# First-unit queries and keys written on chip, a Newton inverse root on VectorE, and low parts of the second layer's up weights on GpSimd

## The chip, the cores and the metric

The kernel runs on one core of one Trainium2 chip. The metric is device time in microseconds (us). A core has five engines that run their own instruction streams in program order and meet only at semaphores: TensorE (PE, with weight loads shown as PEld), VectorE (DVE), ScalarE (ACT), GpSimd (POOL) and SyncE (SP, which here only issues DMAs).

## What is computed

Two transformer-like layers on x of shape 4 x 256 x 512, all in float32. Each layer normalises x, and adds to it an attention (32 query heads, 8 key heads, head size 16) and a feed-forward of the normalised x. Layer 0 has full attention and a GELU network of width 2048; layer 1 has causal attention with rotary embedding and a gated SiLU network of width 512.

```python
x = L0_attn_x
xn = _layernorm(x, axis=-1)
x = x + _L0_attn_ref(xn, L0_attn_Wq, L0_attn_Wk, L0_attn_Wv, L0_attn_Wo) + _L0_ffn_ref(xn, L0_ffn_W1, L0_ffn_fc1_bias, L0_ffn_W2, L0_ffn_fc2_bias)
xn = _layernorm(x, axis=-1)
x = x + _L1_attn_ref(xn, L1_attn_w_qkv, L1_attn_b_qkv, L1_attn_w_dense, L1_attn_b_dense) + _L1_ffn_ref(xn, L1_ffn_w12, L1_ffn_b12, L1_ffn_w3, L1_ffn_b3)

def _layernorm(x, axis=-1, eps=1e-05):
    m = jnp.mean(x, axis=axis, keepdims=True)
    v = jnp.var(x, axis=axis, keepdims=True)
    return (x - m) / jnp.sqrt(v + eps)
```

## The kernel before

**Precision by parts.** Each matmul operand of a projection or a feed-forward is kept as a rounded high part and a low part (the exact value minus the rounded one). `three` (L712) makes a product out of three matmuls. Weights arrive in pieces of 128x512: POOL issues the DMA into one of four `raw` buffers (L605), ACT casts it to the high part (L866, step "split"), and a subtraction makes the low part (step "low"). In layer 0 the subtraction for the pieces 0 to 23 of the up weights (`w_up`) is made by POOL (L644). All other low parts are made by DVE (L987). `low_on_dve` decides which engine it is. `w_up` has two slots, so an up piece is split shortly before TensorE needs it.

**Order.** `program_order` writes one list of steps; every engine walks through the list and carries out its own part of each step, in order. The work is cut into 32 units of 8 slots (`unit_slots`). A unit is a batch row n and one of four groups of 8 query heads; units 0 to 15 are layer 0, 16 to 31 layer 1. In a slot stand one step "st" (scores transposed, PE L792 or L795; exponential by ACT L931 into `probs`; in layer 1 a causal mask on `probs` by POOL, L654) and one step "m" for a later unit (scores, PE L766; their row maximum by DVE, L1086 or L1081). Around them the function `spread` deals out the projections, up, down and out matmuls (L712). "pv" (L814) multiplies probs by the values; it needs the masks of four slots. `followers` puts the "low" step one slot after its "split": for layer 1's up pieces, the split stands in slot 5 and the low in slot 6. "plus" (POOL L669) adds a bias into `x_res`, in units whose group is 3.

**Start.** ACT zeroes part of `q_sb` for the units 0 and 1 ("fill", L869, two casts of 32x2048), then takes the root of the variance. The layer norm is: "stats" on DVE (L997 to L1002), "root" on ACT (L876, Sqrt), "rstd" on DVE (L1008 to L1012, a reciprocal and one Newton step), "ln" on DVE (L1019). TensorE then transposes xn (L732). Keys and queries of batch row 0 go from the projection's bank to `stage`, by DMA to HBM ("store", L556 and L560), and by DMA into `q_sb` and `k_sb` ("load_q" L569, "load_k" L578); the scores of unit 0 wait for both.

**PSUM.** Five banks (`WORK_BANKS`) are handed round among m, qkv, up, down, wo and transposes. A bank comes free only when its reader (mostly DVE) is done.

## Time and profile before

| | |
|---|---|
| device time, median of 3 runs | 614.59 us (612.11 to 616.9) |
| time of the profiled execution | 612.6 us |
| span from its first to its last instruction | 610.8 us |
| PE busy | 568.8 us (93%) |
| PEld busy | 437.6 us (72%) |
| DVE busy | 452.1 us (74%) |
| ACT busy | 363.0 us (59%) |
| POOL busy | 232.5 us (38%) |
| mean granted TensorE clock | 0.989 |

PE is the engine with the least idle time, so what counts is what makes PE wait, and where its clock is granted at less than full. In the views below, a row of a timeline has the start, the duration, the engine, the line, the operation, the output <- the inputs, the shapes and the count; in square brackets stands how long the engine sat idle before it, and what ended that. Rows of the same operation that follow each other without a gap are merged. SPq and POOLq rows are DMA issues.

### The profile page before, as it was taken

The page shows a single profiled execution, that of the slowest core. Times are in us where ns is not written, and L with a number is a line of the kernel's source. Part 1 is how long each engine was busy: PE and PEld are TensorE (multiplying, and loading weights), DVE is VectorE, ACT ScalarE, POOL GpSimd, SP SyncE. Part 2 cuts the span into 40 slices and gives each one's busy share as a digit, 9 for nine tenths or more (in the row PEclk, how much of TensorE's full clock was granted, in tenths as well). Part 3 has the DMA queues.
Part 4 walks back from the last instruction along what each step waited for, and adds up shares of the span by engine and source line. Part 5 has one row for each costly group of instructions (what it writes and reads, how often), then busy time and mean ns, then how long its engine had stood idle before and what let it go on. Part 6 is the DMA issues. An engine that isn't in the chain of part 4 may idle for free.

```text
span 610.8 us, 10473 instructions
## 1 busy us (share of the span) xinstructions
PE 568.8 (93%) x3216; PEld 437.6 (72%) x3216; DVE 452.1 (74%) x1196; ACT 363.0 (59%) x615; POOL 232.5 (38%) x345
## 2 busy tenths in 40 slices
PE   2889899999999999999999998989889999999997
PEld 2786677787777878767777676857667777776764
DVE  5469867756565776476898677888988889798673
ACT  6448756754555674675684665447755664556461
POOL 6303334532303522213223114335755386455242
PEclk9989999999999999999999999979999999998999
DMA  5784632353223244316434324324543355444101
GB/s 190 224 252 129 172 90 68 105 156 105 69 87 105 71 120 140 87 35 173 122 122 121 87 57 118 88 76 120 151 107 88 81 160 143 104 123 105 35 2 69
DMA packets 30247, 68.07 MB, mean 111 GB/s; under 512 B 4848, under 2 KB 17648, under 8 KB 28144
## 3 DMA queue, kind: packets, MB, share of 16 engines
q1 hardware_dynamic: 21552, 39.09, 23.0%
q0 software_dynamic: 8640, 28.32, 15.8%
q8 instruction: 26, 0.43, 0.3%
q14 instruction: 29, 0.24, 0.1%
HBM read 52.44 MB, written 14.68 MB: 110 GB/s over the span
## 4 chain that ended last, share of the span: by engine, by line
PE 73%; ACT 7%; DVE 6%; issue 6%; POOL 5%; DMA 4%; ACTq 0%; SPq 0%; DVEq 0%; POOLq 0%
PE banks L712 50%; PE banks L766 7%; PE banks L792 7%; PE banks L814 6%; DMA q_sb<-max_t 1%; ACT L931 1%; POOL probs L654 1%; DVE banks L1081 1%; PE banks L795 1%; PE banks L732 1%; POOL raw L605 1%; ACT hid_f L951 1%; ACT L950 1%; DMA raw<-in_attn 1%; DMA q_sb<-q_parts 1%
## 5 line engine op out<-in xcount | busy, mean ns | idle before, releaser
L931 ACT ACTIVATE probs<-banks 128x512 f32<-128x512 f32 (+1 forms) x256 | 137.7, 546 | 175.7 <-PE banks L792 141.6
L712 PE MATMUL banks<-xnT,w_up 128*128 128x512 f32 x576 | 152.0, 397 | 1.6 <-issue 1.6
L1086 DVE TENSOR_REDUCE neg_max<-banks 128x2 f32<-128x512 f32 x128 | 87.4, 687 | 87.1 <-PE banks L766 86.7
L712 PE MATMUL banks<-w_down,hid 128*128 128x512 f32 x480 | 128.4, 401 | 4.5 <-ACT hid_f L951 2.0
L712 PEld LDWEIGHTS banks<-xnT,w_up 128*128 128x128 f32 x576 | 101.6, 189 | 29.2 <-issue 12.8
L766 PEld LDWEIGHTS banks<-k_sb,q_sb 96*128 96x128 f32 x512 | 94.3, 195 | 22.5 <-issue 4.1
L1081 DVE CUSTOM_DVE_ANT_0 banks<-banks,mask_qk 128x128 f32<-128x128 f32 (+1 forms) x256 | 86.3, 375 | 32.0 <-PE banks L766 31.9
L712 PEld LDWEIGHTS banks<-w_down,hid 128*128 128x128 f32 x480 | 85.5, 189 | 32.2 <-DVE neg_max L1086 7.5
L766 PE MATMUL banks<-k_sb,q_sb 96*128 96x256 f32 (+1 forms) x512 | 101.0, 279 | 4.7 <-DMA q_sb<-q_parts 3.0
L654 POOL TENSOR_SCALAR_AFFINE_SELECT probs<-probs 128x256 f32<-128x256 f32 x128 | 59.9, 468 | 89.2 <-ACT probs L931 83.1
L792 PE MATMUL banks<-q_sb,k_sb 97*128 97x512 f32 x192 | 80.0, 416 | 11.2 <-ACT probs L931 8.7
L712 PE MATMUL banks<-xnT,w_qkv 128*128 128x256 f32 x576 | 82.4, 291 | 1.6 <-DVE xnT L1025 1.4
L712 PEld LDWEIGHTS banks<-xnT,w_qkv 128*128 128x128 f32 x576 | 75.9, 196 | 4.4 <-DVE xnT L1025 1.8
L1125 DVE TENSOR_TENSOR x_res<-x_res,banks 128x512 f32<-128x512 f32 x96 | 63.7, 676 | 9.5 <-PE banks L712 9.5
L814 PE MATMUL banks<-probs,v_sb 128*32 128x512 f32 (+1 forms) x512 | 61.8, 555 | 1.2 <-POOL probs L654 1.2
L605 POOL DMA_DIRECT2D raw<-in_down x40 | 22.4, 561 | 100.8 <-DVE w_down L987 73.4
L644 POOL TENSOR_TENSOR w_up<-raw,w_up 128x512 fp32r<-128x512 f32 x24 | 32.4, 1350 | 73.3 <-ACT w_up L866 73.1
L792 PEld LDWEIGHTS banks<-q_sb,k_sb 97*128 97x128 f32 x192 | 36.5, 190 | 29.0 <-ACT probs L931 18.6
L712 PE MATMUL banks<-w_out,ctxT 128*128 128x512 f32 x192 | 50.8, 406 | 0.0
L605 POOL DMA_DIRECT2D raw<-in_up x48 | 27.1, 564 | 50.9 <-DVE w_qkv L987 21.6
L712 PEld LDWEIGHTS banks<-w_out,ctxT 128*128 128x128 f32 x192 | 35.1, 193 | 9.4 <-issue 2.9
L931 ACT ACT_TABLE_LOAD x29 | 37.2, 1283 | 0.5
(75 smaller groups left out, 663.1 us busy)
## 6 DMA issues: line engine op xcount, KB each, us to landing
q_sb<-q_parts SPq DMA_DIRECT2D x64, 256.0 KB, 4.5
raw<-in_up POOLq DMA_DIRECT2D x48, 256.0 KB, 3.2
raw<-in_down POOLq DMA_DIRECT2D x40, 256.0 KB, 3.0
q_parts<-stage SPq DMA_DIRECT2D x32, 256.0 KB, 2.5
raw<-in_attn POOLq DMA_DIRECT2D x20, 256.0 KB, 3.2
k_parts<-stage SPq DMA_DIRECT2D x16, 256.0 KB, 2.6
k_sb<-k_parts SPq DMA_DIRECT2D x16, 256.0 KB, 4.4
out<-x_res SPq DMA_DIRECT2D x8, 256.0 KB, 2.1
```

What stands on the lines that cost most here:

```text
L605: pool.dma_start(raw[:, k % RAW, :], src).then_inc(raw_loaded[k % RAW], 16)
L644: nc.gpsimd.tensor_tensor(to[1], raw[:, k % RAW, :], to[0].bitcast(F32), ALU.subtract).then_inc(lo_split_pool, 1)
L654: nc.gpsimd.affine_select(out=tri, in_=tri, compare_op=ALU.is_ge, fill=0.0, base=0, pattern=[[0, 2], [1, P]], channel_multiplier=-1).then_ ...
L712: mm = nc.tensor.matmul(out_ap, lhs(a), rhs(b_), start=first and j == 0, stop=stop and j == 2, **kw)
L732: mm = nc.tensor.transpose(banks[:, k, c * P:c * P + P], xn[:, t, c * P:c * P + P], ident[:, :])
L766: mm = nc.tensor.matmul(banks[:, k, r * T:r * T + w], q_sb[0:ROWS, u % RING, 2 * g + r, t * P:t * P + P], k_sb[0:ROWS, 4 * f + g, 0:w], st ...
L792: mm = nc.tensor.matmul(bank, keys, q_sb[0:MROW + 1, u % RING, 2 * g:2 * g + 2, :], start=True, stop=True)
L814: mm = nc.tensor.matmul(o, v_sb[:, t, 4 * f + g, :], p_, start=t == 0, stop=t == 1, skip_group_check=True)
L931: nc.scalar.activation(probs[:, i, 0:w], banks[:, ST_BANKS[k % 2], 0:w], ACT.Exp, scale=SCALES[n // B]).then_inc(exp_done, 1)
L1081: ins = nc.vector.tensor_tensor_reduce(out=scores, in0=scores, in1=mask_qk[:, T - w:], scale=1.0, scalar=3.0 * MASKED, op0=ALU.add, op1=AL ...
L1086: nc.vector.tensor_reduce(neg_max[:, s, 2 * g:2 * g + 2, t], banks[:, bank_of[x], :].rearrange("p (r t) -> p r t", r=2)[:, :, 0:w], AX.X, ...
L1125: nc.vector.tensor_tensor(x_res[:, tile, :], x_res[:, tile, :], banks[:, bank_of[y], :], ALU.add).then_inc(wk_emptied, 1)
```

## The change

- The first DMAs of keys and queries (stores of batch row 0, pair 2 and pair 0) go from `stage` straight into `k_sb` and `q_sb` (4 and 8 DMAs of 16 partitions x 8 x 256), instead of to HBM and back. "load_k" of row 0 and "load_q" of the units 0 and 1 are gone. Whoever used the HBM copies now waits for `first_k` and `first_q`.
- The fills of units 0 and 1 stand after the splits of the second pair of weight pieces, behind the first root.
- The root on ACT stays only for the first two layer norms. For the other six, DVE makes the inverse root alone: two integer instructions for a first guess and three Newton steps of three instructions.
- The low parts of all 16 up pieces of layer 1, and nothing else, move from DVE to POOL.
- POOL issues the weight loads 4 and 5 before its last three start-up instructions instead of after them.

```diff
 def start_slots():
-    o = [[("fill", 0), ("fill", 1), ("stats", 0, 0), ("root", 0, 0), ("rstd", 0, 0), ("ln", 0)] + split(0, "attn", 4, 5)]
-    o += [[("xn", 0, 0), ("xn", 0, 1)] + split(0, "attn", 0, 1)]
+    o = [[("stats", 0, 0), ("root", 0, 0), ("rstd", 0, 0), ("ln", 0)] + split(0, "attn", 4, 5)]
+    o += [[("xn", 0, 0), ("xn", 0, 1)] + split(0, "attn", 0, 1) + [("fill", 0), ("fill", 1)]]
...
-    o += [[("xn", 1, 0), ("xn", 1, 1), ("fill", 2), ("load_k", 0, 0), ("load_k", 0, 1), ("load_q", 0), ("load_q", 1)] + split(0, "up", 0, 1)]
+    o += [[("xn", 1, 0), ("xn", 1, 1), ("fill", 2)] + split(0, "up", 0, 1)]
...
-        slots[4] += [("root", 0, 2), ("root", 0, 3)]
...
-        slots[5].append(("root", 1, c))
...
-    return x[1] == 1 or x[2] != "up" or x[3] >= 24
+    return x[2] != "up" or x[1] == 0 and x[3] >= 24
...
+                    if x == ("store", 0, 2):
+                        for h in range(2):
+                            for e in range(2):
+                                at = 32 * h + 16 * e
+                                sp_.dma_start(k_sb[at:at + HD, :, :].bitcast(F32),
+                                              stage[:, k % 2, h, 0, :].bitcast(F32)).then_inc(first_k, 16)
+                    elif x == ("store", 0, 0):
+                        for j in range(2):
+                            for e in range(2):
+                                for h in range(2):
+                                    at = 32 * e + 16 * h
+                                    sp_.dma_start(q_sb[at:at + HD, j, :, :].bitcast(F32),
+                                                  stage[:, k % 2, h, j, :].bitcast(F32)).then_inc(first_q[j], 16)
...
             nc.gpsimd.memset(v_sb[:, :, :, :], 1.0).then_inc(made, 1)
             pool.wait_ge(made, ONES_V)
+            load(4)
+            load(5)
             nc.gpsimd.memset(k_sb[MROW:MROW + 1, :, :].bitcast(F32), 1.0).then_inc(made, 1)
...
-                        pe.wait_ge(q_loaded[u % RING], 32 * (u // RING + 1))
-                        pe.wait_ge(k_loaded[f], 16 * (n + 1))
+                        if u < 2:
+                            pe.wait_ge(first_q[u], 64)
+                        else:
+                            pe.wait_ge(q_loaded[u % RING], 32 * (u // RING + u % RING // 2))
...
+                if x[0] == "rstd" and ("stats",) + x[1:] not in stt:
+                    tiles = stat_tiles(x)
+                    t = slice(tiles[0], tiles[-1] + 1)
+
+                    link(nc.vector.tensor_scalar(dev[:, t].bitcast(I32), var_e[:, t].bitcast(I32), 1, None, ALU.arith_shift_right))
+                    link(nc.vector.tensor_scalar(rstd[:, t].bitcast(I32), dev[:, t].bitcast(I32), -1, GUESS, ALU.mult, ALU.add))
+                    for _ in range(3):
+                        link(nc.vector.tensor_tensor(rs0[:, t], rstd[:, t], rstd[:, t], ALU.mult))
+                        link(nc.vector.scalar_tensor_tensor(out=rs1[:, t], in0=rs0[:, t], scalar=-0.5, in1=var_e[:, t],
+                                                            op0=ALU.mult, op1=ALU.mult))
+                        link(nc.vector.scalar_tensor_tensor(out=rstd[:, t], in0=rs1[:, t], scalar=1.5, in1=rstd[:, t],
+                                                            op0=ALU.add, op1=ALU.mult))
```

The order of TensorE's instructions is the same before and after. Three places of the other engines follow.

ACT at the start of the program, before (`dev` is the root of the variance, `q_sb<-zero` are the fills):

```order
L869 ACT_TABLE_LOAD
L869 CAST q_sb<-zero 32x2048 x2
L876 ACT_TABLE_LOAD
L876 ACTIVATE dev<-var_e 128x2
L866 CAST w_qkv<-raw 128x512 x2
L884 CAST xnT<-banks 128x4x128 x2
```

and of the change:

```order
L913 ACT_TABLE_LOAD
L913 ACTIVATE dev<-var_e 128x2
L903 CAST w_qkv<-raw 128x512 x2
L921 CAST xnT<-banks 128x4x128 x2
L903 CAST w_qkv<-raw 128x512 x2
L906 CAST q_sb<-zero 32x2048 x2
L913 ACTIVATE dev<-var_e 128x2
```

The two fills and one table load have gone from ahead of the first root; the fills now stand ahead of the second one.

ACT in unit 16, the first of layer 1, before (L931 is the exponential of the scores):

```order
L969 CAST hid<-hid_f 128x512
L939 CAST ctxT<-o_t 128x256
L876 ACT_TABLE_LOAD
L876 ACTIVATE dev<-var_e 128x2
L866 CAST w_up<-raw 128x512
L931 ACT_TABLE_LOAD
L931 ACTIVATE probs<-banks 128x256 x2
```

and of the change:

```order
L1005 CAST hid<-hid_f 128x512
L975 CAST ctxT<-o_t 128x256
L903 CAST w_up<-raw 128x512
L967 ACTIVATE probs<-banks 128x256 x2
```

The root and both table loads around it are gone; the same happens in the units 0, 8, 12 and 20.

POOL at the end of unit 19, before (L654 is the mask, L676 the low part of the attention's output, L698 that of a key or query):

```order
L669 TENSOR_TENSOR x_res<-x_res,bias_out 128x512
L654 AFFINE_SELECT probs<-probs 128x256
L676 TENSOR_TENSOR ctxT<-o_t,ctxT 128x256
L654 AFFINE_SELECT probs<-probs 128x256
L605 DMA raw<-in_down 128x512
L654 AFFINE_SELECT probs<-probs 128x256
```

and of the change:

```order
L700 TENSOR_TENSOR x_res<-x_res,bias_out 128x512
L685 AFFINE_SELECT probs<-probs 128x256
L707 TENSOR_TENSOR ctxT<-o_t,ctxT 128x256
L685 AFFINE_SELECT probs<-probs 128x256
L675 TENSOR_TENSOR w_up<-raw,w_up 128x512
L634 DMA raw<-in_down 128x512
L685 AFFINE_SELECT probs<-probs 128x256
```

The low part of the next up piece stands in POOL's queue behind the mask of slot 6 and ahead of the mask of slot 7; before, DVE made it.

## Rows read from the trace of the kernel before

**Rows 1.** Waits of PE: who waited for whom, us in total, times, longest.
```profile
PE banks L792 <- ACT probs L931: 8.7, 6, 2.7
```

**Rows 2.** Timeline of the start: start us, us, engine, line, what.
```profile
2.10 3.69 ACT L869 CAST q_sb<-zero 32x2048 fp32r<-32x2048 f32 x2
...
5.30 0.17 DVE L1002 TENSOR_SCALAR var_e<-mv 128x2 f32<-128x2 f32 x1
...
5.81 1.28 ACT L876 ACT_TABLE_LOAD   x1
...
7.21 1.80 POOL L623 MEMSET k_sb<- 1x2048 f32 x1
...
7.93 1.11 DVE L1011 TENSOR_SCALAR rs<-rs 128x2 f32<-128x2 f32 x1
...
9.93 1.57 PEld L732 LDWEIGHTS banks<-ident,xn 128*128 128x128 f32 x8 [9.93 <-POOL mask_qk L625]
...
13.30 7.41 PE L712 MATMUL banks<-xnT,w_qkv 128*128 128x256 f32 x48 [1.40 <-DVE xnT L1025]
```

**Rows 3.** Timeline of the first scores (unit 0).
```profile
26.72 1.75 SPq L569 DMA_DIRECT2D q_sb<-q_parts  x4
...
32.34 0.47 PE L766 MATMUL banks<-k_sb,q_sb 96*128 96x256 f32 x2 [3.04 <-DMA q_sb<-q_parts]
...
38.34 0.52 PE L712 MATMUL banks<-xnT,w_qkv 128*128 128x256 f32 x3
...
38.94 1.56 PE L712 MATMUL banks<-xnT,w_up 128*128 128x512 f32 x6
```

**Rows 4.** Timeline of unit 0, slots 6 and 7.
```profile
57.72 1.28 ACT L876 ACT_TABLE_LOAD   x1
...
62.30 0.50 PE L792 MATMUL banks<-q_sb,k_sb 97*128 97x512 f32 x1 [2.40 <-ACT probs L931]
...
68.67 0.62 ACT L866 CAST w_out<-raw 128x512 fp32r<-128x512 f32 x1 [3.61 <-DMA raw<-in_attn]
```

**Rows 5.** Timeline of unit 16's end and unit 17's start.
```profile
395.81 1.28 ACT L876 ACT_TABLE_LOAD   x1
...
399.57 0.79 PE L792 MATMUL banks<-q_sb,k_sb 97*128 97x512 f32 x1 [2.69 <-ACT probs L931]
...
405.92 1.57 PE L712 MATMUL banks<-w_out,ctxT 128*128 128x512 f32 x6
```

**Rows 6.** Timeline of the same steps at unit 20's end, PE.
```profile
459.54 0.50 PE L792 MATMUL banks<-q_sb,k_sb 97*128 97x512 f32 x1 [0.67 <-ACT probs L931]
...
463.23 1.09 PE L712 MATMUL banks<-w_out,ctxT 128*128 128x512 f32 x4
```

**Rows 7.** Windows: us, busy (x) of PE, PEld, DVE, ACT, POOL, PEclk, DMA, GB/s.
```profile
34.00:36.00 2.00, 2.00 (x11) 2.00 (x10) 1.45 (x3) 0.00 (x0) 0.00 (x0) 0.50 0.82 302
...
210.00:250.00 40.00, 40.00 (x222) 31.06 (x221) 25.54 (x50) 23.59 (x38) 11.94 (x16) 1.00 0.40 118
...
345.00:611.00 266.00, 247.40 (x1472) 187.16 (x1470) 212.70 (x761) 148.69 (x275) 121.62 (x201) 0.98 0.35 95
...
401.00:403.00 2.00, 2.00 (x6) 1.60 (x5) 1.97 (x5) 0.01 (x1) 1.69 (x2) 0.50 0.47 131
```

**Rows 8.** Groups by line: busy us, mean ns, idle before and its releasers.
```profile
L644 POOL TENSOR_TENSOR w_up<-raw,w_up 128x512 fp32r<-128x512 f32 x24 | 32.4, 1350 | 73.3 <-ACT w_up L866 73.1
...
L987 DVE TENSOR_TENSOR w_up<-raw,w_up 128x512 fp32r<-128x512 f32 x24 | 17.9, 763 | 1.4 <-ACT w_up L866 1.4
```

**Rows 9.** Timeline where unit 24 begins: a low part, its use, the mask before it.
```profile
499.15 1.29 POOL L669 TENSOR_TENSOR x_res<-x_res,bias_out 128x512 f32<-128x512 f32 x1 [0.17 <-POOL probs L654]
...
499.52 1.48 DVE L987 TENSOR_TENSOR w_up<-raw,w_up 128x512 fp32r<-128x512 f32 x1
...
502.26 1.09 PE L712 MATMUL banks<-xnT,w_up 128*128 128x512 f32 x4
502.27 0.41 POOL L654 TENSOR_SCALAR_AFFINE_SELECT probs<-probs 128x256 f32<-128x256 f32 x1
```

More of the change, by code:

```diff
@@ L10 @@
 BF16 = mybir.dt.bfloat16
+I32 = mybir.dt.int32
 ALU = mybir.AluOpType
@@ L32 @@
 MASKED = -1e38
+GUESS = 0x5F3759DF
 CHUNKS = (2048 // P, 512 // P)
@@ L336, in build @@
     stg = numbered(order, "store")
-    stt = numbered(order, "stats")
+    stt = {("stats",) + x[1:]: k for x, k in numbered(order, "root").items()}
     ups = numbered(order, "up")
@@ L432, in build @@
         m_loaded = [sem(f"m_loaded{k}") for k in range(RING)]
+        first_k = sem("first_k")
+        first_q = [sem(f"first_q{j}") for j in range(2)]
         st_filled = sem("st_filled")
@@ L460, in unit, with wait_stored, wait_stage_free @@
             return n, s, s // 2
+        def wait_stored(eng, k):
+            eng.wait_ge(staged[k % 2], 32 * (k // 2))
+        def wait_stage_free(eng, k):
+            if k == 2:
+                eng.wait_ge(first_k, 64)
+            elif k == 3:
+                for j in range(2):
+                    eng.wait_ge(first_q[j], 64)
+            elif k > 3:
+                wait_stored(eng, k - 2)
         def wait_fill_read(eng, x):
@@ L552, in _ @@
                         sp_.wait_ge(staged_lo, rounds[("qkv", n, pair)] + 1)
-                    if pair < 2:
+                    if x == ("store", 0, 2):
[5 more added lines that the diff above has]
+                    elif x == ("store", 0, 0):
+                        for j in range(2):
+                            for e in range(2):
[3 more added lines that the diff above has]
+                                                  stage[:, k % 2, h, j, :].bitcast(F32)).then_inc(first_q[j], 16)
+                    elif pair < 2:
                         for j in range(2):
@@ L573, in _ @@
                     k = stg[("store", n, 2)]
[L574 removed]
+                    wait_stored(sp_, k)
                     if n:
@@ L1001, in _ @@
                     t = slice(tiles[0], tiles[-1] + 1)
-                    nc.vector.tensor_scalar(var_e[:, t], mv[:, t, 1], EPS, None, ALU.add).then_inc(var_ready, 1)
-                if x[0] == "rstd":
+                    ins = nc.vector.tensor_scalar(var_e[:, t], mv[:, t, 1], EPS, None, ALU.add)
+                    if x in stt:
+                        ins.then_inc(var_ready, 1)
+                    else:
+                        link(ins)
+                if x[0] == "rstd" and ("stats",) + x[1:] not in stt:
[9 more added lines that the diff above has]
+                                                            op0=ALU.add, op1=ALU.mult))
+                elif x[0] == "rstd":
                     k = stt[("stats",) + x[1:]]
```

14 lines of the change are left out of this document (8 added, 6 removed).

## The prediction

> **What bounds the kernel.** I read the waits of PE first. PE is busy for 93% of the span, so only what it waits for can be won, and the clock that it is granted meanwhile. Its largest entry that the change can touch is 8.7 us for the exponential on ACT, in 6 waits [rows 1]. Then I read the timeline at each large wait. The first is the start: PE's first weight load stands at 9.93 [rows 2]. The second is the wait of 3.04 at 32.34, for unit 0's queries [rows 3]. The third and fourth are waits of 2.40 at 62.30 and 2.69 at 399.57, each behind a root on ACT [rows 4, 5]. The windows tell what a wait costs beyond itself: at 34 to 36 us, after the wait of 3.04, and at 401 to 403 us, after that of 2.69, the granted clock is 0.50, the lower level of 1.2 GHz [rows 7]. In layer 1 (345 to 611 us) DVE is busy for 212.70 of 266 us, PE for 247.40 and POOL for 121.62 [rows 7]: DVE is PE's close second there, POOL has room on average.
>
> **The start, part by part.** The variance is ready at 5.47 (5.30 + 0.17), but ACT has only just finished the fills and loads its table until 7.09 [rows 2]. With the fills behind it and the table loaded while x arrives, the root runs at 5.5 instead of 7.1: 1.6 us. Next, one tiny DVE instruction of the chain (L1011) lasts 1.11 us and ends at 9.04, when POOL's memset (7.21 + 1.80 = 9.01) ends [rows 2]; its like need 0.17. The change puts two loads that wait for DVE ahead of that memset and so takes it out of the chain: 0.94 more. PE would begin at 9.93 - 2.54 = 7.4. A half microsecond memset of `v_sb` could lie across the chain instead, so the bounds are 2.0 and 2.54; I take 2.5. The fills (3.69 us) now stand before the second root. The casts ahead of them should end near 11, the fills near 14.8, and the second layer norm some 2.2 later, at 17.0. PE is busy with projections until 20.71 - 2.5 = 18.2 (13.30 + 7.41) [rows 2]: hidden, with about 1 us to spare; without it that us is lost.
>
> **First queries.** Before, four loads are issued from 26.72 on, behind the stores; the first scores start at 32.34, after the wait of 3.04 [rows 3]. Now the 8 DMAs follow the queries' low part directly, near 19.5, and at 0.44 us an issue (1.75 / 4, [rows 3]) the four of unit 0 are issued by 21.3. Before, 5.6 us passed from the first issue to the use (32.34 - 26.72). The same makes 25.1 now, or 26.9 counted from the last issue, and PE arrives at 32.34 - 3.04 - 2.5 = 26.8. So 3.0 us are won, at worst 2.9. The eight rounds of scores behind the wait last 6.6 us (32.34 to 38.94), while the last of them takes 0.60 (38.34 to 38.94) [rows 3]; with no wait ahead of them the clock should stay at 2.4 GHz, and they take 8 x 0.6 = 4.8, or 5.0 with DVE's maxima behind them: 1.6 us.
>
> **Roots in the middle.** At five places two table loads of 1.28 and a root of 0.2 go. In unit 0 the wait of 2.40 goes, but 6 us later ACT waits 3.61 for a weight DMA whose issue hangs on a cast that now comes only 1.5 earlier [rows 4]. I take 1.5 (bounds -1 and 2.4: DVE has no idle time in these slots, and its part grows, below). In unit 16 the wait of 2.69 shrinks to about 0.2, since the exponentials follow one cast instead of two loads. Behind it PE needs 6.35 us (399.57 to 405.92) for the steps that at the end of unit 20 take 3.69 (459.54 to 463.23) [rows 5, 6]: that is the low clock, 2.66 us. Together 5.1. In unit 20 the wait is 0.67 [rows 6]; I take 0.6. Unit 8's place lies in a window where PE is busy for 40.00 of 40 us [rows 7]; nothing is won there, and I take unit 12's as the same.
>
> **Newton steps.** Six times 11 dependent instructions replace 5. At 0.20 us each (0.17 and the way to the next) that is 1.2 us more of DVE per place, 7.2 in all. The four single places have PE work queued in four other banks, and cost nothing; the two in unit 0 come back to back (2.4 us) and are in its bounds above. The cover is the spare banks; without it a place costs 1.2.
>
> **Low parts on POOL.** 16 subtractions of 0.76 leave DVE (12.2 us) and cost POOL 1.35 each (21.6 us) [rows 8]. The mean hides the place. The low now queues behind the mask of slot 6. Where unit 24 begins, that mask ends at 502.27 + 0.41 = 502.68, so the low can end at 502.7 + 1.35 = 504.05; PE wants the piece at 502.26 [rows 9]. That is 1.8 us late, because a bias addition of 1.29 on POOL stands ahead (499.15). The same sum for all 16 pieces gives six late ones: 2.1 and 1.8 (after units 19 and 23, which have that addition) and four of 0.1 to 0.5, together 5.3 us. On the other side DVE, which is the close second, sheds 12.2 us, and catches up while PE waits. I take half of the 5.3: 2.6 (bounds: a gain of 1.5, where DVE's relief outweighs it, and a loss of 5.3 and two falls of the clock at 2.66).
>
> What is queued behind a late low on POOL: the mask of slot 7, one weight DMA. Their users wait no longer than PE itself.
>
> A row speaks against this step: DVE's low at 499.52 lasts 1.48 instead of 0.76 on average [rows 8]. It begins while POOL's addition runs (499.15 to 500.44) and ends at 501.00, which is 0.56 after that addition [rows 9]: it seems to have stood still until the addition was nearly or wholly done. The Trainium skill (SBUF — State Buffer, "SBUF: two separate sides") says why: VectorE instructions with two SBUF inputs and GpSimd instructions that read SBUF take one port pair in turns, each for its whole length. By that rule the trace agrees, and every low on POOL may hold DVE; that is rival D.
>
> **The sum.** 2.5 + 3.0 + 1.6 + 1.5 + 5.1 + 0.6 = 14.3 won, 2.6 lost, 11.7 net. The profiled execution took 612.6 (span 610.8 and 1.8 around it), so it would become 600.9; from the median of 614.59, which lies 2.0 above, 602.9. I forecast 602.9.
>
> **Rivals.**
> - **B, late lows cost in full.** The 5.3 add up and the two long ones (1.8 and 2.1) each bring the low clock. For it: a wait of 2.69 did. Against: one of 2.40 in unit 0 did not. 14.3 - 5.3 - 5.3 = 3.7 won: 610.9, within 1%.
> - **C, DVE's relief counts.** Lows cost nothing and layer 1 gains 1.5: 15.8 won, 598.8.
> - **D, slower: port turns.** Each of the 16 lows holds a DVE instruction for up to 1.3 us, and the DVE work is on PE's path. 16 x 1.3 = 20.8, less 12.2 shed, and 5.3 of lateness: 13.9 lost on top of the Newton steps' 7.2, against 14.3 won: 621.4. It decides once each low costs PE more than 0.9 (14.3 / 16). Against: most DVE instructions of layer 1 (L1081, 256 of them) read a bank, not two SBUF tiles, and DVE has 53 us of idle time there.
> - **E, the queries land late.** If the 12 DMAs of 16 partitions are over 1.7 us (26.8 - 25.1) slower than before's loads, PE still waits and the clock still falls. That forfeits up to 4.6: 607.5. The Trainium skill (SBUF — State Buffer, "Door 1: The DMA port swizzle") speaks for it: 16 partitions reach only 4 of 16 ports, measured there as 104 GB/s. No run here shows that width; an estimate by that page is 5 us for 512 KB on one such group, and half where two groups alternate, as here.
>
> **Chances.** Forecast 0.55, C 0.18, B 0.15, E 0.07, D 0.05. About 1% (6 us, 608.4 to 620.7) is what a measurement of this kernel can tell from no change. The forecast's own spread is 599 to 607. Faster: the forecast's 0.55, C's 0.18, E's 0.07, less a little where bounds meet (0.78); within 1%: B and some (0.17); slower: D (0.05). The range leaves out D, B's far end and C's: 597 to 609.
>
> **What would show it.** After: PE's first load at 7.4; no wait for DMA before unit 0's scores, and full clock there; 11 table loads fewer; the place at 399 us (near 389 then) at full clock; waits of PE "issue" or for POOL's `w_up` before up matmuls of layer 1, longest after the units 19 and 23. Wrong would be: PE waiting for DVE in unit 0 for more than 2 us, a clock of 0.5 anywhere behind a late low, DVE's two-input instructions in layer 1 (L1111, L1146) growing by over half.

## The result, and the profile after

The changed kernel is slower. Its median is 620.04 us (619.23 to 622.1, 4 runs) against 614.08 (612.11 to 616.9, 4 runs) for the kernel before: a ratio of 1.011, 95% interval 1.0067 to 1.0154. The forecast was 602.9, range 597 to 609.

| | after |
|---|---|
| time of the profiled execution | 619.58 us |
| span | 617.6 us |
| PE busy | 573.9 us (93%) |
| DVE busy | 449.3 us (73%) |
| ACT busy | 348.9 us (56%) |
| POOL busy | 253.1 us (41%) |
| mean granted TensorE clock | 0.986 |

TensorE runs the same 3216 matmuls in the same order in both kernels, so each can be laid beside its twin. Start of the same matmul (us), and how far the changed kernel is behind:

```text
matmul no.  before   after    behind   where
0             9.96     7.58   -2.38    first transpose
102          32.34    30.84   -1.50    first scores (wait for queries)
127          36.86    36.31   -0.55
187          45.44    46.61   +1.17    first score tile that needs the maxima of unit 0
259          62.30    60.98   -1.32    where the root of unit 0 was waited for
291          69.84    70.44   +0.60
1453        289.55   291.03   +1.48
2044        399.57   399.64   +0.07    where the root of unit 16 was waited for
2065        405.68   403.06   -2.62
2121        416.02   415.52   -0.50
2374        459.54   461.25   +1.71
2610        498.45   501.41   +2.96
3215        607.21   614.06   +6.85    last
```

So three things happen. The start's gain is gone by 47 us. The layer norms' gain comes and partly goes again. From 416 us on the changed kernel loses 7.3 us, in steps, most of them at the late low parts. The waits of PE in the changed kernel (engine, tile, line, what ended the wait: us in total, times, longest) say for what:

```profile
PE banks L829 <- DMA q_sb<-max_t: 5.5, 9, 1.2
PE banks L743 <- DVE neg_max L1133: 5.1, 4, 1.5
...
PE banks L803 <- DMA q_sb<-stage: 2.7, 1, 2.7
...
PE banks L803 <- DVE neg_max L1138: 1.7, 1, 1.7
```

The 8.7 us for the exponential [rows 1] have become 0.8. In their place stand the transfer of the maxima (`max_t`, 5.5), four waits of 5.1 at L743 that the profile gives to DVE, and 1.7 for a row maximum. Those four are late low parts. DVE had finished; what ended last was POOL's subtraction. A fifth late one makes a wait of 0.52 at 429.64, which the profile calls "issue": its subtraction ends at 429.54. Here is one of the four, from the changed kernel's timeline at the start of unit 20:

```profile
441.23 0.63 ACT L903 CAST w_up<-raw 128x512 fp32r<-128x512 f32 x1
...
441.43 1.30 POOL L700 TENSOR_TENSOR x_res<-x_res,bias_out 128x512 f32<-128x512 f32 x1 [0.17 <-POOL probs L685]
...
443.41 0.72 POOL L707 TENSOR_TENSOR ctxT<-o_t,ctxT 128x256 fp32r<-128x256 f32 x1
...
444.27 0.41 POOL L685 TENSOR_SCALAR_AFFINE_SELECT probs<-probs 128x256 f32<-128x256 f32 x1
...
444.83 1.27 POOL L675 TENSOR_TENSOR w_up<-raw,w_up 128x512 fp32r<-128x512 f32 x1
...
446.19 2.25 PE L743 MATMUL banks<-xnT,w_up 128*128 128x512 f32 x6 [1.38 <-DVE neg_max L1133]
```

The cast ends at 441.86, but the low part starts at 444.83, behind the bias addition, the low part of the attention's output and two masks (one of them, at 442.86, not shown), and ends at 446.10. PE starts 0.09 us later. The six matmuls then take 2.25 us where at full clock they take 1.6.

The clock is in the windows of the changed kernel (us; busy and count of PE, PEld, DVE, ACT, POOL; granted clock; DMA share; GB/s):

```profile
31.00:36.00 5.00, 5.00 (x24) 5.00 (x25) 2.86 (x5) 0.00 (x0) 0.00 (x0) 0.50 1.05 214
...
401.00:403.00 2.00, 2.00 (x16) 1.27 (x15) 1.76 (x8) 0.60 (x1) 1.69 (x4) 1.00 0.69 160
...
446.00:452.00 6.00, 5.80 (x26) 4.08 (x27) 2.93 (x12) 1.20 (x2) 3.06 (x7) 0.72 0.37 89
...
562.00:568.00 6.00, 6.00 (x29) 4.42 (x28) 3.66 (x16) 1.80 (x3) 1.48 (x4) 0.63 0.22 51
```

After the wait for the first queries the clock is 0.50, the level of 1.2 GHz, still. At 401 to 403 us, where it was 0.50 [rows 7], it is now 1.00. It falls again behind two of the late low parts: it is 0.50 from 447 to 450 us, and from 560 to 566. But not every late one brings it: behind the longest wait, 1.49 at 506.87, it stayed 1.00. And the second fall is not all new. The kernel before, which has no late low part there, has a shorter one close by (0.50 from 553 to 555):

```profile
552.00:558.00 6.00, 5.60 (x27) 4.36 (x28) 4.49 (x21) 3.00 (x8) 3.64 (x7) 0.72 0.75 195
```

### The profile page after: what moved, and what is told of

Same layout as the page of the kernel before. It is cut to its first block, busy times and chain, and to the rows that moved or that the text cites. A ratio compares the mean times of both kernels' runs of the same rounds, so it can differ in the third digit from the quotient of the medians.

```text
span 617.6 us, 10513 instructions
## 1 busy us (share of the span) xinstructions
PE 573.9 (93%) x3216; PEld 440.0 (71%) x3216; DVE 449.3 (73%) x1216; ACT 348.9 (56%) x598; POOL 253.1 (41%) x361
## 4 chain that ended last, share of the span: by engine, by line
PE 71%; DVE 11%; issue 6%; DMA 5%; ACT 4%; POOL 2%; SPq 0%; DVEq 0%; ACTq 0%; POOLq 0%
PE banks L743 48%; PE banks L803 7%; PE banks L851 6%; PE banks L829 6%; DMA q_sb<-max_t 2%; DVE banks L1133 2%; DMA q_sb<-stage 1%; PE banks L832 1%; DVE bn L1033 1%; PE banks L763 1%; ACT hid_f L987 1%; DVE x_res L1177 1%; DVE neg_max L1133 1%; ACT L986 1%; POOL probs L685 1%
## 5 line engine op out<-in xcount | busy, mean ns | idle before, releaser
L743 PE MATMUL banks<-xnT,w_up 128*128 128x512 f32 x576 | 153.6, 400 | 7.4 <-DVE neg_max L1133 5.1
L743 PE MATMUL banks<-w_down,hid 128*128 128x512 f32 x480 | 127.7, 400 | 4.5 <-ACT hid_f L987 2.0
L743 PEld LDWEIGHTS banks<-xnT,w_up 128*128 128x128 f32 x576 | 102.1, 190 | 35.9 <-issue 12.8
L743 PEld LDWEIGHTS banks<-w_down,hid 128*128 128x128 f32 x480 | 85.1, 188 | 32.2 <-DVE neg_max L1138 7.5
L685 POOL TENSOR_SCALAR_AFFINE_SELECT probs<-probs 128x256 f32<-128x256 f32 x128 | 58.4, 456 | 73.0 <-ACT probs L967 66.2
L675 POOL TENSOR_TENSOR w_up<-raw,w_up 128x512 fp32r<-128x512 f32 x40 | 55.2, 1380 | 77.6 <-ACT w_up L903 75.3
L743 PE MATMUL banks<-xnT,w_qkv 128*128 128x256 f32 x576 | 84.4, 295 | 1.6 <-DVE xnT L1077 1.4
L743 PEld LDWEIGHTS banks<-xnT,w_qkv 128*128 128x128 f32 x576 | 78.1, 201 | 4.4 <-DVE xnT L1077 1.8
L743 PE MATMUL banks<-w_out,ctxT 128*128 128x512 f32 x192 | 49.6, 398 | 0.0
L743 PEld LDWEIGHTS banks<-w_out,ctxT 128*128 128x128 f32 x192 | 34.3, 189 | 9.2 <-issue 2.9
L707 POOL TENSOR_TENSOR ctxT<-o_t,ctxT 128x256 fp32r<-128x256 f32 x32 | 24.0, 750 | 30.2 <-ACT ctxT L975 28.3
```

The source lines that it names most:

```text
L675: nc.gpsimd.tensor_tensor(to[1], raw[:, k % RAW, :], to[0].bitcast(F32), ALU.subtract).then_inc(lo_split_pool, 1)
L685: nc.gpsimd.affine_select(out=tri, in_=tri, compare_op=ALU.is_ge, fill=0.0, base=0, pattern=[[0, 2], [1, P]], channel_multiplier=-1).then_ ...
L707: nc.gpsimd.tensor_tensor(ctxT[:, 1, s, :], o_t[:, :], ctxT[:, 0, s, :].bitcast(F32), ALU.subtract).then_inc(ctx_lo, 1)
L743: mm = nc.tensor.matmul(out_ap, lhs(a), rhs(b_), start=first and j == 0, stop=stop and j == 2, **kw)
```

## The experiments

Names of the parts, used below: **fills** (the moved fills and POOL's two loads), **queries** (the first keys and queries on chip), **roots** (Newton on DVE), **lows** (the second layer's up low parts on POOL). Every kernel here computes the whole reference. The ratio is to the kernel before, measured on the same chip; its median was 613.6 in the first eight runs, 613.1 in the next four and 613.9 in the last two.

| kernel | median | ratio | interval |
|---|---|---|---|
| all but lows | 613.15 | 0.9989 | 0.9961 to 1.0017 |
| lows only | 620.72 | 1.0115 | 1.0079 to 1.0151 |
| roots only | 611.68 | 0.9971 | 0.9938 to 1.0003 |
| queries only | 617.22 | 1.0050 | 1.0024 to 1.0075 |
| fills and roots | 610.60 | 0.9953 | 0.9931 to 0.9975 |
| lows, split one slot earlier | 616.39 | 1.0047 | 1.0025 to 1.0069 |
| split one slot earlier only | 624.01 | 1.0183 | 1.0146 to 1.0221 |
| keys only on chip | 613.43 | 1.0004 | 0.9976 to 1.0032 |
| lows, low next to its cast | 616.04 | 1.0037 | 1.0013 to 1.0061 |
| fills, roots, six lows | 610.37 | 0.9946 | 0.9921 to 0.9971 |
| fills, roots but unit 0's on ACT | 610.70 | 0.9941 | 0.9916 to 0.9966 |
| keys and unit 0's queries on chip | 613.89 | 1.0004 | 0.9981 to 1.0026 |
| fills only | 612.92 | 0.9986 | 0.9958 to 1.0014 |
| fills, roots, keys and unit 0's queries | 611.69 | 0.9965 | 0.9944 to 0.9985 |

### Which part costs what

**All but lows.** From the changed kernel, one line goes back:

```diff
-    return x[2] != "up" or x[1] == 0 and x[3] >= 24
+    return x[1] == 1 or x[2] != "up" or x[3] >= 24
```

> The changed kernel with one part undone: the low parts of the second layer's up pieces are back on VectorE; fills, first queries and Newton roots stay as changed. Theory L (late lows): comparing the two traces, the changed kernel is 0.5 us ahead of the kernel before at 436 us and 6.9 behind at the end, and between them stand six waits of TensorE of 0.9 to 1.5 us for a piece's second form, so the lows cost 7.4 us: expected 619.6 - 7.4 = 612.2 by the profile, a ratio of 0.997 to the kernel before (0.994 to 1.000). Theory S (the late queries and roots are the larger loss, and the lows only inherit it): the lows cost 2.6 as predicted, and this kernel takes 617, a ratio of 1.004 or more.

Measured: 0.9989. **Lows only** is the same line turned round, in the kernel before.

> The kernel before with one part of the change: the low parts of the second layer's up pieces on GpSimd. Theory L: the lows cost 7.4 us by themselves, time 621.5 (619 to 623), ratio 1.012, with TensorE's waits of 0.9 to 1.5 us ahead of matmuls on a piece's second form in units 18 to 29. Theory S: 2 to 3 us, 617, ratio 1.004. If the relief of VectorE that the prediction put against the late lows is real, less than 2 us, ratio under 1.003.

Measured: 1.0115, which is 7.1 us. Both kernels say the same: theory L. The lows alone make the kernel slower, and without them the change is a draw. The waits of PE in the lows-only kernel have the same four as the changed kernel:

```profile
PE banks L712 <- DVE neg_max L1081: 5.2, 4, 1.5
```

The fifth, of 0.51, is there too. That leaves 7.1 - 5.2 - 0.5 = 1.4 us. The clock that falls behind them is one part of it; the masks are another. They stand behind the low parts in POOL's queue, and PE's "pv" waits for them, in the lows-only kernel and in the kernel before:

```profile
PE banks L814 <- POOL probs L654: 2.7, 5, 1.0
```

```profile
PE banks L814 <- POOL probs L654: 1.2, 2, 0.9
```

How the 1.4 us divide between the two is not shown.

**Roots only.** The kernel before with the Newton part of the diff.

> The kernel before with only the Newton roots in place of ScalarE's (units 0 and the four places of the first layer that prepare the second layer). Theory N (the roots pay late only): in unit 0 the run of 24 small VectorE instructions takes the place of the 2.40 us that TensorE lost to the root, 0 to +2 us there; at unit 16 the wait of 2.69 falls to the next one (a transfer), and the full clock pays about 2.5 more, -3.9; sum about -2 to -3, ratio 0.995 to 0.997. The prediction's terms: 1.5 + 5.1 + 0.6 = -7.2, ratio 0.988. If unit 0's run holds up what it holds up in the changed kernel (+3.3 from 61 to 79 us) and the gain of unit 16 is given back within the unit, +0 to +1, ratio 1.000 to 1.002.

Measured: 0.9971, so 1.8 us won, with an interval from 3.8 won to 0.2 lost. Theory N holds and the prediction's 7.2 does not. The same matmuls, laid beside those of before in the profiled executions, are 0.1 us behind at 289 us: nothing was won in unit 0. They are 4.2 ahead at 401.5 and 2.4 ahead at 457: that is what unit 16 leaves, and unit 20 adds nothing. This kernel's timeline of PE at unit 16 shows what took the root's place:

```profile
398.10 0.47 PE L792 MATMUL banks<-q_sb,k_sb 97*128 97x512 f32 x1 [1.04 <-DMA q_sb<-max_t]
...
408.81 0.27 PE L775 MATMUL banks<-ident,neg_max 128*16 128x128 f32 x1 [1.16 <-DVE neg_max L1097]
```

The wait of 2.69 [rows 5] became one of 1.04 for the maxima's transfer. Ten us later PE waits 1.16 for DVE. On DVE the Newton run stands ahead of that, and ends at 402.22 (DVE's timeline, same kernel):

```profile
400.27 1.23 DVE L1017 SCALAR_TENSOR_TENSOR rstd<-rs,rstd 128x2 f32<-128x2 f32 x1
...
402.06 0.16 DVE L1017 SCALAR_TENSOR_TENSOR rstd<-rs,rstd 128x2 f32<-128x2 f32 x1
```

From there to PE's wait DVE is never idle for 0.2 us. One instruction of the run took 1.23 us instead of 0.16, so this place cost DVE about 3.2 us and not 2.2. It ends at 401.50, when a product on POOL ends (401.47):

```profile
400.20 1.27 POOL L688 TENSOR_TENSOR rot_a<-qkv_v,table 128x512 f32<-128x512 f32 x1 [0.17 <-POOL probs L654]
```

The clock at this place is less certain than one pair of profiles makes it look. Seven profiled kernels keep ACT's root here and have the same wait of 2.7 us for it. The 21 matmuls from that wait to the first scores of the next unit took 6.1 us in the kernel before, 4.9 to 5.0 in five (lows only, queries only, low next to its cast, keys and unit 0's queries, fills only), and 3.4 in keys only, which is what they take with the Newton root. There the clock did not fall at all. From the timeline and a window of keys only:

```profile
401.21 0.50 PE L813 MATMUL banks<-q_sb,k_sb 97*128 97x512 f32 x1 [2.67 <-ACT probs L951]
```

```profile
402.00:404.00 2.00, 2.00 (x17) 1.48 (x15) 1.86 (x6) 1.04 (x3) 1.69 (x4) 1.00 0.47 129
```

So the clock behind that wait cost 0 to 2.7 us, 1.5 on average of the seven.

**Queries only.** The kernel before with the first keys and queries on chip.

> The kernel before with only the first queries and keys sent on chip, with its fills where they were. Theory Q (the 12 small transfers on one queue are slower than the trip through DRAM saves, since each issue took 0.65 us and they land 7.9 us after): from the changed kernel's trace the start loses 3 us from the first scores to the end of the first maxima, where the prediction gained 4.6: ratio 1.003 to 1.005. The prediction's own step: -3.0 for the queries and -1.6 for the clock, ratio 0.992. A third way: the issue is slow in the changed kernel only because its weights' transfers start earlier there (the fills moved); then this one gains 2 to 3 us, ratio 0.996.

Measured: 1.0050, 3.1 us lost (1.5 to 4.6). Theory Q. The third way, that the moved fills are what makes the transfers slow, is out, since the fills are where they were. SyncE's queue in this kernel:

```profile
19.21 2.64 SPq L573 DMA_DIRECT2D k_sb<-stage  x4
22.29 5.11 SPq L580 DMA_DIRECT2D q_sb<-stage  x8
```

An issue takes 0.64 to 0.66 us, where the prediction took 0.44. But the issue is not the whole cost. Windows of the kernel before:

```profile
25.00:30.00 5.00, 2.99 (x12) 2.17 (x12) 0.82 (x2) 0.88 (x2) 3.65 (x4) 1.00 0.92 244
30.00:35.00 5.00, 2.66 (x17) 2.69 (x18) 1.97 (x3) 0.00 (x0) 0.00 (x0) 0.85 0.99 252
```

and of the queries-only kernel:

```profile
25.00:30.00 5.00, 2.98 (x12) 2.17 (x12) 1.03 (x2) 1.19 (x3) 3.69 (x4) 1.00 1.13 140
30.00:35.00 5.00, 3.03 (x25) 3.06 (x26) 2.52 (x5) 0.00 (x0) 0.00 (x0) 1.00 1.12 157
```

The DMA engines show as busy nearly throughout in both (a share of 0.92 to 1.13, which adds up the time of packets and so can pass 1), and move 140 to 157 GB/s instead of 244 to 252. Fewer bytes are moved, but each costs more. The size of the packets is not what makes the difference to the stores: in the traces a packet of 1 KB took 52 ns on average in the stores to HBM (kernel before, 23 to 27 us) and 129 in the transfers on chip (25 to 30 us). What stands behind them is late too. The DMA issues from 15 to 50 us of this kernel (KB each, median us to landing):

```profile
q_sb<-stage SPq DMA_DIRECT2D x8, 128.0 KB, 7.7
...
raw<-in_down POOLq DMA_DIRECT2D x2, 256.0 KB, 9.5
...
q_sb<-max_t SPq DMA_DIRECT2D x1, 8.0 KB, 5.7
```

and the timeline of PE there:

```profile
31.97 0.48 PE L801 MATMUL banks<-k_sb,q_sb 96*128 96x256 f32 x2 [2.45 <-DMA q_sb<-stage]
...
47.85 0.77 PE L827 MATMUL banks<-q_sb,k_sb 97*128 97x512 f32 x1 [3.62 <-DMA q_sb<-max_t]
```

The first scores start 0.37 us earlier than before (31.97 against 32.34), and no more. The loss is taken at 47.85, where the 8 KB of the maxima came late: they land after 5.7 us, against 3.3 in the kernel before, where PE did not wait for them. Behind this wait the clock falls, and not behind the one at 31.97. A window of this kernel:

```profile
48.00:51.00 3.00, 3.00 (x9) 2.42 (x10) 1.29 (x2) 0.60 (x1) 1.52 (x2) 0.50 1.02 393
```

**Keys only**, and **keys and unit 0's queries**, send 4 and 8 of the 12 transfers on chip, the rest through HBM.

In "keys only" the branch for the store of pair 0 is taken out, and its semaphores with it. "Unit 0's" has this in its place:

```diff
+                        for e in range(2):
+                            for h in range(2):
+                                at = 32 * e + 16 * h
+                                sp_.dma_start(q_sb[at:at + HD, 0, :, :].bitcast(F32),
+                                              stage[:, k % 2, h, 0, :].bitcast(F32)).then_inc(first_q[0], 16)
+                        dst = qscr[0, 1].rearrange("(h d) (g t) -> (d g) h t", h=2, g=UH)
+                        sp_.dma_start(dst, stage[:, k % 2, :, 1, :].bitcast(F32)).then_inc(first_q[1], 16)
+                        sp_.wait_ge(first_q[1], 16)
+                        for e in range(2):
+                            sp_.dma_start(q_sb[32 * e:32 * e + 32, 1, :, :].rearrange("p g t -> p (g t)").bitcast(F32),
+                                          qscr[0, 1]).then_inc(first_q[1], 16)
```

> The kernel before with only the first keys sent on chip (4 of the 12 transfers) and the queries through DRAM. Theory R (rate): the transfers into 16 partitions occupy all DMA engines at 140 to 180 GB/s where those through DRAM ran at 240 to 300, so the 8 of the queries, 1.0 MB, hold the queue and what is behind it 5 us longer; with the keys alone the traffic is 0.5 MB instead of 1.0 MB at half the rate, about even: ratio 0.997 to 1.001. Theory I (issue): 12 issues of 0.65 us hold SyncE; four cost 1.2 us: ratio 1.001 to 1.003.

> The kernel before with the keys and only unit 0's queries sent on chip (8 transfers of 128 KB), unit 1's through DRAM (one store, two loads). Theory R: half of the queries' slow traffic goes, but its trip through DRAM stands behind it in the queue; a loss of 1 to 2 us, ratio 1.001 to 1.004. If the count of SyncE's issues is what costs, 11 issues instead of 12: as with all on chip, ratio 1.004 to 1.006. If what the direct way was meant for works once the queue is lighter (scores earlier by 3 us), ratio 0.995 to 0.998.

Measured: 1.0004 and 1.0004. Four transfers cost nothing that can be measured, nor do eight (by the intervals at most 2.0 and 1.6 us); twelve cost 3.1 us. The unit 0 kernel has 11 issues like the full one's 12, so theory I falls. It moves unit 1's half of the queries the fast way, and the maxima land after 4.9 us instead of 5.7. Its median came out better than theory R's 1 to 2 us, though the interval reaches into them; PE still waits 2.31 us for the maxima there. That the rate itself comes from the 16 partitions of each transfer was not varied on its own. That these transfers end in on-chip memory and not in HBM is a rival for it, which no run here tells apart.

**Fills only**, from the kernel before:

```diff
-    IDENT, K_ZERO, ONES_V, ALL_MADE, EARLY = 3, 4, 5, 8, 4
+    IDENT, K_ZERO, ONES_V, ALL_MADE, EARLY = 3, 4, 5, 8, 6
```

with the fills one slot later and the loads 4 and 5 ahead of POOL's memset of `k_sb`.

> The kernel before with only the fills of the 0/1 matrices and GpSimd's two loads moved. Theory F (the start's gain ends where the queries arrive): in the trace of fills with Newton roots TensorE is 2.40 us ahead at its first load and 0.23 ahead when the first scores start, which wait for the queries in both; so 0 to 1 us is left: ratio 0.998 to 1.000. The prediction's term, 2.5 won in full: 0.996.

Measured: 0.9986 (2.6 won to 0.9 lost). Its timeline of PE:

```profile
7.58 1.94 PE L734 MATMUL banks<-ident,xn 128*128 128x128 f32 x8 [7.58 <-DVE xn L1021]
...
32.02 0.77 PE L768 MATMUL banks<-k_sb,q_sb 96*128 96x256 f32 x2 [4.79 <-DMA q_sb<-q_parts]
```

PE starts 2.38 us earlier, and waits 4.79 instead of 3.04 [rows 3] for the queries. The result lies within theory F: most of a start is lost where the next transfer lands when it did.

The single parts add up: -0.9 (fills) - 1.8 (roots) + 3.1 (queries) + 7.1 (lows) = +7.5 us, and the whole change measured 1.011 x 614 - 614 = +6.8.

### Why the lows cost 7 us

**Low next to its cast.** In the lows-only kernel, POOL takes the low part right after its cast in the order, nothing else moves:

```diff
-        return [(1, ("low", x))]
+        return [(0 if x[1:3] == (1, "up") else 1, ("low", x))]
```

> Lows on GpSimd as in the lows-only kernel; casts, transfers and all else where they were, but GpSimd takes each low of a second-layer up piece next after its cast, ahead of one or two masks instead of behind them. Theory P (place in the queue: in the lows-only trace, piece 37 was cast by 441.87 and its low began at 444.81, behind two masks that waited for exponentials): 2 to 3 us of lateness go at each of the six pieces on which TensorE waited, so most of the 7.1 us: 614 to 615.5, ratio 1.000 to 1.003; what is left is the masks held 1.3 us longer. Theory D (the two engines' accesses to SBUF): lows stay at up to 2.5 us and the masks behind them are late instead: 618 or more, ratio over 1.006.

Measured: 1.0037. Of 7.1 us, 4.8 are gone with the place in the queue: mostly theory P. The rest is 2.3 us (0.8 to 3.7). In the profiled execution three of the 16 pieces still end 0.1 us before PE starts on them: two behind one of POOL's bias additions, and one at 557.72 behind the low part of the attention's output alone. PE's waits in front of these three are 0.98, 0.94 and 0.39 us, 2.3 together. This kernel's POOL timeline at the first of them:

```profile
439.73 1.28 POOL L669 TENSOR_TENSOR x_res<-x_res,bias_out 128x512 f32<-128x512 f32 x1 [0.17 <-POOL probs L654]
...
442.58 1.27 POOL L644 TENSOR_TENSOR w_up<-raw,w_up 128x512 fp32r<-128x512 f32 x1
```

**Split one slot earlier**, with the lows on POOL, and, as its control, with the lows on DVE:

```diff
-        slots[5] += split(1, "up", v + 2)
+        slots[4] += split(1, "up", v + 2)
```

> Lows on GpSimd as in the lows-only kernel, and in units 16 to 28 the piece's cast and with it its low part one slot (1.5 to 2 us) earlier in every queue. If the lows cost 7.1 us because they end 1 to 1.5 us after TensorE wants them (place in GpSimd's queue), they are then in time: 613.5, ratio 0.997 to 1.002. If they cost because GpSimd's subtract and VectorE's work on SBUF hold each other up (2.5 us for one instead of 1.3 us), moving them changes little: 618 or more, ratio over 1.006.

> The control to the run above: the kernel before with the same one-slot move and the lows on VectorE. In the trace of before, TensorE's uses of a piece follow its low part by 0.1 to 2.2 us, so the pieces are nearly late there too: if that costs anything now, this gains up to 2 us (ratio 0.997 to 0.999); otherwise no change (0.999 to 1.002). If the earlier cast delays ScalarE's exponentials, which release TensorE, a loss of up to 2 us (1.001 to 1.003).

Measured: 1.0047 and 1.0183. The control is the surprise: a cast and a low part 2 us earlier, and 11.2 us lost. No expectation for it came near. In its waits of PE the maxima's transfer stands first, with 16.9 us in 12 waits (2.4 in 7 before). One of the 12, of 2.7 us at unit 16, was ACT's before; the rest is new or longer:

```profile
PE banks L792 <- DMA q_sb<-max_t: 16.9, 12, 2.7
```

and its timeline shows how:

```profile
520.36 0.59 POOL L605 DMA_DIRECT2D raw<-in_down  x1 [0.84 <-DVE w_up L987]
...
520.88 0.51 SPq L585 DMA_DIRECT2D q_sb<-max_t  x1
```

A freed `raw` buffer lets POOL issue the next weight load. That load of 256 KB now starts 0.5 us ahead of the 8 KB of the maxima, and shares the DMA engines with it. Before, the pair stood at 511.75 (maxima) and 514.20 (weights). The median landing of `max_t` between 400 and 600 us is 2.7 us in the control, and 1.8 in the kernel before:

```profile
q_sb<-max_t SPq DMA_DIRECT2D x13, 8.0 KB, 2.7
```

```profile
q_sb<-max_t SPq DMA_DIRECT2D x14, 8.0 KB, 1.8
```

With the lows on POOL the load is issued later (516.63, behind the maxima at 515.59), the landing is 1.8 again, and the loss is 2.9. So this pair doesn't tell lateness from the rest as it was meant to. The run above does.

**Fills, roots and six lows.** Only the pieces with slack go to POOL:

```diff
-    return x[1] == 1 or x[2] != "up" or x[3] >= 24
+    return x[2] != "up" or x[3] >= 24 if x[1] == 0 else x[2] != "up" or x[3] not in (0, 1, 2, 6, 10, 14)
```

> The kernel before with fills and Newton roots (measured at a ratio of 0.995), and only six of the sixteen lows on GpSimd: those that ended 3.4 us or more ahead of TensorE's use when all sixteen were there. Theory L: no wait is left, and VectorE's relief pays nothing to 1 us: ratio 0.993 to 0.996. If GpSimd's low costs by being there (slows VectorE, moves the weights' transfers into the window of the maxima's transfer), it costs six sixteenths of 7.1 us: ratio 1.000.

Measured: 0.9946, beside 0.9953 for fills and roots alone. Low parts on POOL that are in time cost nothing, and DVE's relief pays nothing, that can be measured (either interval is about 1.5 us to each side). Only six of the 16 were moved here, so it tests the relief of 4.6 us of DVE's time (6 x 0.76), not of all 12.2.

**Do the two engines hold each other up?** At one piece, yes. The changed kernel's timeline:

```profile
489.13 2.50 POOL L675 TENSOR_TENSOR w_up<-raw,w_up 128x512 fp32r<-128x512 f32 x1
489.23 1.28 DVE L1023 TENSOR_TENSOR w_down<-raw,w_down 128x512 fp32r<-128x512 f32 x2
...
491.74 1.63 PE L743 MATMUL banks<-xnT,w_up 128*128 128x512 f32 x6 [1.32 <-DVE neg_max L1133]
```

POOL's subtraction takes 2.50 us, of which DVE's two subtractions fill 1.28; the other 1.22 is about what it takes alone. That agrees with the Trainium skill (SBUF — State Buffer, "SBUF: two separate sides"): the two take the shared port pair in turns. By the profile POOL starts 0.10 us first and is the one held; spans on POOL are rough, so these rows do not show which of the two goes first. The hold made the wait of 1.32. But DVE's own two-input instructions, which rival D needed, hardly grew: 545 ns against 588, and 790 against 730. Mean ns from 345 to 600 us in the changed kernel:

```profile
L1163 DVE TENSOR_TENSOR o_div<-o_tok,o_rec 128x256 f32<-128x256 f32 x17 | 9.3, 545 | 0.6
L1198 DVE TENSOR_TENSOR hid<-hid_f,hid 128x512 fp32r<-128x512 f32 x10 | 7.9, 790 | 1.1 <-ACT hid L1005 1.1
```

and in the kernel before:

```profile
L1111 DVE TENSOR_TENSOR o_div<-o_tok,o_rec 128x256 f32<-128x256 f32 x18 | 10.6, 588 | 0.6
...
L1146 DVE TENSOR_TENSOR hid<-hid_f,hid 128x512 fp32r<-128x512 f32 x10 | 7.3, 730 | 1.1 <-ACT hid L969 1.1
```

### What is worth keeping

**Fills and roots**: the diff without its queries and lows.

> The kernel before with the fills and GpSimd's two loads moved and the Newton roots; queries through DRAM, lows on VectorE. Additive theory: the single parts measured so far are lows +7.1, roots -1.9, queries +3.6, and all but the lows -0.5, so the fills give -0.5 - 3.6 + 1.9 = -2.2, and this kernel takes 613.6 - 2.2 - 1.9 = 609.5, ratio 0.993 (0.990 to 0.996). Rival: the start's gain is eaten by the queries' trip through DRAM, which is then no earlier than now: ratio 0.997, that of the roots alone.

**Unit 0's root back on ACT**, on top of it:

```diff
+        slots[4] += [("root", 0, 2), ("root", 0, 3)]
         slots[6] += [("rstd", 0, 2), ("rstd", 0, 3)]
```

> The kernel before with fills and Newton roots, but unit 0's root back on ScalarE. Theory: unit 0's run of 24 VectorE instructions (5.6 us) costs as much as the root's 2.40 us wait did (in the trace of the Newton-only kernel, TensorE is 2.4 us ahead at 59.9 and 0.7 behind at 67.1), so nothing changes or it gains 1: ratio 0.993 to 0.996. The prediction's term for this place (1.5 won): this kernel is 1.5 us slower than with all roots on VectorE, ratio 0.998.

**With keys and unit 0's queries on chip**, on fills and roots:

> Fills, Newton roots, keys and unit 0's queries on chip, unit 1's queries through DRAM, lows on VectorE. If the parts add (fills and roots 0.995, the lighter on-chip way 1.000): 0.995. If the start 2.4 us earlier now reaches the scores, since what the first scores wait for also starts earlier: 0.990 to 0.993, a version that beats both kernels by more than the fills and roots alone. If the heavier traffic meets the weights' transfers that GpSimd now asks for earlier: 0.998 to 1.000.

Measured: 0.9953, 0.9941 and 0.9965. Fills and roots beat both kernels: 610.60 is 2.9 us under the kernel before, measured beside it, and 9.4 under the changed kernel's median. For fills and roots the rival's 0.997 lies just inside the interval. Whose root makes unit 0's layer norm makes no difference that these runs can tell. The lighter way on chip does not turn the early start into time: in its timeline the first scores start at 31.92, after a wait of 3.82 for the queries.

```profile
31.92 0.77 PE L808 MATMUL banks<-k_sb,q_sb 96*128 96x256 f32 x2 [3.82 <-DMA q_sb<-stage]
```

## Why the prediction was wrong

The forecast was 11.7 us won; by the medians 6.0 were lost. Two steps of it had the wrong sign or size by several us: the queries, whose new transfers were priced by the time of other ones, and the low parts, whose lateness was halved for a relief of DVE that did not come. The roots gave a quarter of their term, and the start a third.

| term | predicted, us won | measured alone, us won |
|---|---|---|
| start (fills) | 2.5 | 0.9 (-0.9 to 2.6) |
| queries and the clock behind them | 3.0 + 1.6 | -3.1 (-4.6 to -1.5) |
| roots | 1.5 + 5.1 + 0.6 | 1.8 (-0.2 to 3.8) |
| lows | -2.6 | -7.1 (-9.3 to -4.8) |
| sum | 11.7 | -7.5 |

- **Start: the step was right, the term not.** PE's first matmul came at 7.58 (9.96 before); forecast was a load at 7.4. But the term was taken in full because the queries were to be on chip by 25.1. They were not. In the fills-only kernel PE waited 4.79 instead of 3.04 us for them, and began the scores 0.3 ahead.
- **Queries: wrong, the largest miss.** The first of the eight issues was forecast near 19.5 and came at 20.91. "At 0.44 us an issue" and "5.6 us passed from the first issue to the use" were taken from other transfers: loads from HBM into 32 partitions. The new ones took 0.65 an issue, and 9.9 us passed in the changed kernel from the first issue (20.91) to the use (30.84). The first scores won 0.4 us without the fills. The clock was predicted at full and was 0.50 from 31 to 36. The step also asked only when the queries arrive, and not what stands behind them: the maxima's transfer landed after 5.7 us and cost PE 3.62.
- The clock was the smaller part of it, and not where the prediction had it: in the queries-only kernel it stayed 1.00 behind the first scores and fell to 0.50 behind the maxima's wait.
- This is **rival E**'s mechanism, held at 0.07. Its bound for a loss was the whole gain given back, 4.6; it was 3.1 beyond that. The Trainium skill (SBUF — State Buffer, "Door 1: The DMA port swizzle") says that 16 partitions reach 4 of 16 ports. The measured 140 to 157 GB/s at full DMA share, with other transfers in the mix, agree in direction. The rule deserved more than 0.07, since no row of before had such a transfer.
- **Roots: the waits went, the time did not all come.** The wait at 399 us shrank from 2.69 to 1.04, not to 0.2: behind the exponential stood the maxima's transfer. The 2.66 us of clock came in full in this pair of profiles (1.00 at 401 to 403), but it was read from one execution: over the seven kernels with the same wait the clock cost 1.5 on average. Then 1.7 were given back at a wait of 1.16 for DVE, since "the four single places have PE work queued in four other banks, and cost nothing" was wrong for the transpose of the maxima, which needs DVE's last maximum and nothing else. In unit 0 nothing was won, where 1.5 was taken; that lay inside its bounds. The changed kernel's timeline there:

```profile
61.82 1.47 DVE L1047 TENSOR_SCALAR dev<-var_e 128x2 int32<-128x2 int32 x1
...
61.95 1.30 POOL L675 TENSOR_TENSOR w_up<-raw,w_up 128x512 fp32r<-128x512 f32 x1
...
67.27 0.16 DVE L1053 SCALAR_TENSOR_TENSOR rstd<-rs,rstd 128x2 f32<-128x2 f32 x1
67.47 0.69 DVE L1138 TENSOR_REDUCE neg_max<-banks 128x2 f32<-128x512 f32 x1
...
68.21 0.50 PE L803 MATMUL banks<-k_sb,q_sb 96*128 96x256 f32 x2 [1.66 <-DVE neg_max L1138]
```

The first Newton instruction lasts until POOL's subtraction ends (63.29 and 63.25), and the two runs take 5.6 us (61.82 to 67.43), not 4.4. PE waits for the row maximum behind them.
- **Lows: the lateness was right, what it costs was halved.** The "six late ones", "together 5.3 us", came out as six pieces that end 0.1 us before their use, four waits of 5.1 us and a fifth of 0.5. The waits behind the units 19 and 23 were forecast at 2.1 and 1.8 and measured 1.38 and 1.49. "I take half" had no row behind it. The relief of DVE, the reason for the half, was nothing that can be measured, and falls of the clock came on top (0.50 from 447 to 450 us, and from 560 to 566, where part of it was there before). "Their users wait no longer than PE itself" was wrong as well: PE's waits for masks rose from 1.2 to 2.7 us in the lows-only kernel. **Rival B** had the sum 5.3 + 5.3 = 10.6; it was 7.1. Of its two long waits one brought the low clock (1.38, at 446.19) and the longer one did not (1.49).
- **Rival C** (relief) showed no worth with six low parts: 0.9946 against 0.9953. **Rival D** was right that the two engines take turns, and wrong that it decides: one wait of 1.32 in 16 pieces. Where DVE was held in PE's path, it was the Newton steps, which D did not name: by POOL's subtraction at 61.82, and in unit 16 twice (at 399.48 for 1.15 us by the moved low part, and at 402.69 for 1.23 by POOL's L719). What these holds cost PE was not measured alone.
- Of the tests that the prediction set, PE's first load, the 11 table loads fewer (60 and 49), the clock at 399 us and the longest waits behind the units 19 and 23 came true. "no wait for DMA before unit 0's scores" failed first, at 30.84. Of its signs of being wrong one came: a clock of 0.50 behind a late low part, at 446.9.

Open is how the loss of the low parts beyond PE's waits for them, 1.4 us of 7.1, divides between clock and masks, and whether the low rate of the transfers on chip comes from their 16 partitions. The last 2.3 us of the low parts next to their casts are as much as PE waits in front of the three pieces that still end late; no run moved those three alone.

## What to carry to other kernels

Price a new transfer by its own shape. The ones into 16 partitions held the DMA engines 1.6 to 1.8 times as long per byte moved as the traffic through HBM, and the price is paid by whatever small transfer the bottleneck waits for next. Before work goes to a less busy engine, read its place in that engine's queue at each use: the mean load did not show it, and the lateness cost TensorE its full time here, with clock and masks on top. A won wait is worth only the distance to the next thing that lands when it did before.

## What was not expected of the hardware

- A fall of TensorE's clock does not follow from the length of the wait alone. Behind waits of 2.72 and 3.82 us for the first queries it was 0.50; in the queries-only kernel, behind 2.45 at the same place, 1.00. Behind a wait of 1.38 (446 us) it was 0.72 over six us, and behind one of 1.49 (507 us) 1.00. And behind the same wait of 2.67 to 2.69 at unit 16 the same 21 matmuls took 6.1, 4.9 to 5.0, or 3.4 us in seven kernels. A gain of clock that is read from one profile is one draw.
- An 8 KB transfer on TensorE's path landed after 1.8 us alone and 2.7 in the median when a 256 KB load was issued half a microsecond ahead of it or less than 0.1 behind (single ones up to 3.5). With the load 0.6 to 0.9 us behind it landed after 1.8. PE's waits for it rose by 14.5 us, of which 2.7 had been ACT's.
- The start varies between executions: with the same start in the code, the wait for the first queries was 3.0, 3.3, 3.7, 4.1 and 4.2 us (kernels before, low next to its cast, lows only, and the two with the split earlier). A difference of 1 us there in two single profiles shows nothing.
